# Causal masks as stack rows and small triangles, value products over two slots

## What is computed

```python
# L0 cross (its own half is causal), L2 feed-forward's attention
att = jnp.where(causal[None, None], att, -jnp.inf)
# L2 attention: three passes, each output is the next query
mask = jnp.triu(jnp.full((S, S), -10000.0), 1)
scores = jnp.einsum('bthd,bshd->bhts', q, k * scale) + mask
for _ in range(REPETITIONS - 1):
    context = _self_attention(context, k, v, mask)
```

## Time and profile before

| | |
|---|---|
| three runs | 4332.91, 4342.0, 4346.76 us, median 4342.0 |
| the profiled execution | span 4397.2 us; the time around it isn't shown, and it is an execution of its own beside the three |
| mean granted TensorE clock | 0.867 |
| busy over the span | PE 78%, PEld 51%, DVE 64%, ACT 47%, POOL 27% |
| instructions | 86721 |

### The profile page before, as it was taken

One profiled execution on the slowest core, in us unless ns is written; L12 is line 12 of the kernel. 1 busy time (PEld: TensorE's weight loads), 2 busy tenths in 40 slices (PEclk: granted clock), 3 DMA queues, 4 the chain that ended last, 5 costly groups with the idle time before them and its releaser, 6 DMA issues. The chain is left out here.

```text
span 4397.2 us, 86721 instructions
## 1 busy us (share of the span) xinstructions
PE 3437.7 (78%) x30670; PEld 2240.3 (51%) x30670; DVE 2793.4 (64%) x7633; ACT 2088.0 (47%) x4656; POOL 1182.3 (27%) x2276
## 2 busy tenths in 40 slices
PE   6886888896888658759998989677993588869882
PEld 2443554463555338734454545343553466669882
DVE  5884675264786575547676777476865468954453
ACT  2664665232443435426666766443660234335551
POOL 2322221011111234540101110133322422234555
PEclk9987998797998679969999999787995599879996
DMA  5323331033221322230202021223322230122322
GB/s 89 64 35 55 56 56 22 15 95 49 32 39 14 57 70 67 76 58 21 42 24 38 25 38 27 37 53 54 55 35 65 80 92 19 59 70 85 91 80 62
DMA packets 320664, 231.40 MB, mean 53 GB/s; under 512 B 45491, under 2 KB 305168, under 8 KB 320188
## 3 DMA queue, kind: packets, MB, share of 16 engines
q1 hardware_dynamic: 306444, 198.57, 22.8%
q0 software_dynamic: 12928, 26.50, 2.1%
q10 hardware_dynamic: 864, 0.79, 0.1%
HBM read 68.43 MB, written 55.53 MB: 28 GB/s over the span
## 5 line engine op out<-in xcount | busy, mean ns | idle before, releaser
L1373 ACT ACTIVATE PT<-ps 128x512 f32<-128x512 f32 (+1 forms) x1600 | 812.2, 559 | 468.7 <-PE ps L1433 223.0
L1323 DVE TENSOR_REDUCE M<-ps 128x2 f32<-128x512 f32 x1024 | 655.3, 684 | 236.1 <-PE ps L1307 209.3
L1286 PE MATMUL ps<-SKB 49*128 49x256 bf16 (+2 forms) x3584 | 422.6, 275 | 131.7 <-DVE M L1323 53.5
L1320 DVE TENSOR_REDUCE M<-ps 128x3 f32<-128x384 f32 x768 | 390.6, 550 | 180.5 <-PE ps L1304 119.5
L1468 PE MATMUL ps<-PT,VA 128*9 128x256 f32 (+1 forms) x7168 | 449.8, 370 | 1.3 <-ACT PT L1373 1.0
L3847 ACT ACTIVATE SKB<-ps,SKB 128x128 f32<-128x128 f32 x1032 | 295.5, 372 | 279.6 <-PE ps L3765 194.6
L1413 PE MATMUL ps<-SKB 51*128 51x256 bf16 (+2 forms) x3584 | 362.6, 267 | 59.4 <-DMA SKB<-MT 37.0
L3911 DVE COPY SKB<-SKB 128x1028 f32 (+1 forms) x258 | 186.6, 723 | 287.0 <-PE ps L3774 167.7
L1286 PEld LDWEIGHTS ps<-SKB 48*128 48x128 bf16 (+1 forms) x3584 | 137.8, 95 | 427.9 <-issue 131.0
L3774 PE MATMUL ps<-SKB 128*128 128x128 f32 x2064 | 288.7, 285 | 29.9 <-ACT SKB L3847 22.1
L3765 PE MATMUL ps<-SKB 128*128 128x128 f32 x2064 | 293.4, 288 | 0.0
(11 more groups left out here) (497 smaller groups left out, 6720.8 us busy)
## 6 DMA issues: line engine op xcount, KB each, us to landing
SKB<-HH SPq DMA_DIRECT2D x1212, 64.0 KB
SKB<-HH SPq DMA_DIRECT2D x576, 32.0 KB
PT<-L_sorted_rows SPq DMA_DIRECT2D x258, 64.0 KB
L_sorted_results<-SKB SPq DMA_DIRECT2D x258, 64.0 KB
SKB<-in_L3f_w SPq DMA_DIRECT2D x32, 256.0 KB
L_sorted_rows<-TV SPq DMA_DIRECT2D x2, 4032.0 KB, 29.4
SKB<-scratch SPq DMA_DIRECT2D x2, 2048.0 KB, 11.0
SKB<-in_L1f_w SPq DMA_DIRECT2D x16, 256.0 KB
```

Source lines behind the costliest of these rows:

```text
L1286: k = e.matmul(self.mx_bank(m + i)[:, o:o + n], K.QS[self.set(c)][64 * i:64 * i + rows, s, 256 * bb + 128 * qt:256 * bb + 128 * qt + 128], ...
L1320: k = e.tensor_reduce(K.M3[n % 2][:, hh, 0:3], mx[:, 0:384].rearrange("p (a k) -> p a k", a=3), axis=AX.X, op=ALU.max)
L1323: k = e.tensor_reduce(K.M3[n % 2][:, hh, 0:2], mx.rearrange("p (a k) -> p a k", a=2), axis=AX.X, op=ALU.max)
L1373: e.activation(K.PT[:, x % 4, n * i:n * i + n], self.st_bank(x, i)[:, 0:n], ACT.Exp, bias=0.0, scale=self.scale).then_inc(*self.exp.inc())
```

## The change

Masks. Behind the 48 rows of a head's stack come three mask rows, then the two ones rows (shift). Key row j is 0 up to key 64j + 63 and masked behind; query row j is 1 for queries 64j to 64j + 63. So the products that are made anyway mask all but four 64 x 64 triangles on the diagonal. `pe_triangle` adds these: per head two products with 64 rows (the head's own half of the array; an identity shifted by 64 columns in `idh`) and 128 columns, in place of one with 128 rows and 256 columns. The mask of the maxima now stands right behind the maxima. Value products are divided: the first key tile one slot earlier than before, the second where both were.

Copies. The 13 row patterns are made by DVE at the begin in one partition of X, written to DRAM in slot 30 of s0 (`sp_table`), and each stage copies its rows from there ahead of its first three stacks. `sp_mask_rows`, `sp_ones` and the loads of two masks at the begin and of one with the weights of s6 go.

```diff
+        self.idh = [sb(f"idh{i}", [128, 128], BF16) for i in range(2)]
+        self.tri = sb("tri", [128, 4, 64], BF16)
...
+    def sp_table(self, e):
+        K = self.K
+        e.wait_ge(*self.patterns.at(0))
+        for r in range(13):
+            e.dma_start(K.row_table[r:r + 1, :].rearrange("p (b k) -> p b k", b=16),
+                        K.X[0:1, r:r + 1, :].to_broadcast([1, 16, 128])).then_inc(self.tabled.sem, 16)
+
     def sp_rows(self, e, c):
         K = self.K
+        if c == 0:
+            e.wait_ge(*self.tabled.at(0))
...
+        for i, words in enumerate((A["c_maskq"][0:64, 0:32], A["c_maskk"][0:64, 0:32], A["c_addm"][0:64, 0:32],
+                                   A["c_addm"][0:64, 128:160])):
+            for par in range(2):
+                e.dma_start(K.tri[64 * par:64 * par + 64, i, :].bitcast(F32), words).then_inc(self.late.sem, 16)
...
         e.tensor_copy(K.idb[:, :], K.idf[:, :]).then_inc(*self.set.inc())
+        self.dve_patterns(e)
+
+    def dve_patterns(self, e):
+        K = self.K
+        rows = K.X[0:1, 0:13, :].bitcast(BF16)
+        for at, value in ((0, NEG), (5, MASKED)):
+            for j in range(3):
+                e.memset(rows[:, at + j, 0:64 * j + 64], 0.0)
+                e.memset(rows[:, at + j, 64 * j + 64:256], value)
+            e.memset(rows[:, at + 3:at + 5, :], 1.0)
+        for j in range(3):
+            if j > 0:
+                e.memset(rows[:, 10 + j, 0:64 * j], 0.0)
+            e.memset(rows[:, 10 + j, 64 * j:64 * j + 64], 1.0)
+            e.memset(rows[:, 10 + j, 64 * j + 64:256], 0.0)
...
-        self.mrow = 49 if mode == "add" else 48
+        self.mrow = 51 if self.masked else 48
...
+            if step == 0 and key < 3:
+                self.sp_stack_rows(e, kind, key)
...
+    def sp_stack_rows(self, e, kind, c):
+        K, i = self.K, self.set(c)
+        if kind == "q":
+            at, n, dst = 10, 3 * self.masked, K.QS[i]
+        elif self.masked:
+            at, n, dst = 5 * (self.mode == "add"), 5, K.KS[i]
+        else:
+            at, n, dst = 3, 2 * (self.begin is None), K.KS[i]
+        for par in range(2 if n else 0):
+            r = 64 * par + 48
+            e.dma_start(dst[r:r + n, :, :].bitcast(F32), K.row_table[at:at + n, :].rearrange("r (a k) -> r a k", a=8)
+                        ).then_inc(self.rows_in[i].sem, 16)
...
+    def pe_triangle(self, e, bank, i, sub, turned):
+        K = self.K
+        if self.mode == "causal":
+            blocks = bank.rearrange("p (a k) -> p a k", a=2)
+        else:
+            blocks = bank.rearrange("p (a k) -> p a k", a=4)[:, 0:4:3, :]
+        part = slice(64 * i, 64 * i + 64)
+        tri = K.tri[part, 2 * (self.mode == "add") + turned:2 * (self.mode == "add") + turned + 1, :].to_broadcast([64, 2, 64])
+        return e.matmul(blocks[:, :, 64 * sub:64 * sub + 64], K.idh[sub][part, :], tri, start=False, stop=sub == 1)
...
     def pe_max_mask(self, e, u, s):
         K, mode = self.K, self.mode
-        if mode == "none":
+        if self.masked:
+            for sub in range(2):
+                for i in range(2):
+                    k = self.pe_triangle(e, self.mx_bank((16 + 4 * self.cross) * u + 2 * s + i), i, sub, 0)
+                    if sub == 1:
+                        k.then_inc(*self.mx.inc())
+        if mode != "bias":
             return
...
     def pe_exp_mask(self, e, u, s):
...
+        if self.masked:
+            for sub in range(2):
+                for i in self.heads(x):
+                    k = self.pe_triangle(e, self.st_bank(x, i), i, sub, 1)
+                    if sub == 1:
+                        k.then_inc(*self.st.inc())
...
-    def pe_pv(self, e, u, j):
+    def pe_pv(self, e, u, j, kt):
...
-        if j % 2 == 0 and f > 0:
+        if kt == 0 and j % 2 == 0 and f > 0:
             e.wait_ge(*self.tv.at(f - 1))
...
-        e.wait_ge(*self.exp_done(x + 1))
+        if kt == 0:
+            e.wait_ge(*self.exp_done(x + 1))
...
+        if kt == 1:
+            k.then_inc(*self.pv.inc())
...
+        if maxima and self.masked:
+            self.pe_max_mask(e, *maxima)
         if scores:
             self.pe_exp(e, *scores)
-        if maxima:
+        if maxima and not self.masked:
             self.pe_max_mask(e, *maxima)
...
         for j in range(4):
-            u = self.at(g, LE + 2 * j + 3)
-            if u is not None:
-                self.pe_pv(e, u, j)
+            for kt in range(2):
+                u = self.at(g, LE + 2 * j + 2 + kt)
+                if u is not None:
+                    self.pe_pv(e, u, j, kt)
...
+        if self.begin and g == 30:
+            self.begin.sp_table(e)
```

More of the change, by code:

```diff
@@ L929, in sp, with __init__ @@
         e.dma_start(K.BIG[96:100, 0:8192], K.A["c_kc"]).then_inc(self.kone.sem, 16)
-def twice(mask):
-    return mask.rearrange("p (o k) -> p o k", o=1).to_broadcast([128, 2, 128])
 class SelfAttention(Heads):
     LE, MBT, CMBT, TV, GATE = 12, 9, 11, (5, 9, 11), 8
-    def __init__(self, K, prev, W, mode, rope=False, reps=1, gate=False, cross=False, kind="ln", g=None, lead=0, ring=0, again=False,
-                 begin=None):
+    def __init__(self, K, prev, W, mode, rope=False, reps=1, gate=False, cross=False, kind="ln", g=None, lead=0, ring=0, begin=None):
         self.K, self.prev, self.W, self.mode, self.rope = K, prev, W, mode, rope
@@ L974, in __init__ @@
         self.rope_tables = (W["rc"], W["rs"]) if rope else None
-        self.mask = W["mask"].bitcast(BF16) if mode == "add" else None
-        self.mrow = 49 if mode == "add" else 48
+        self.masked = mode in ("causal", "add")
+        self.mrow = 51 if self.masked else 48
         self.MX = (0, 1) if mode == "bias" else (0, 1, 5)
@@ L982, in __init__ @@
         self.scale_q = RS8 / self.scale
-        self.rows_in = K.ev("mask_rows_in", 1, 16 * 18) if mode == "add" else None
-        self.ones_in = K.ev("ks_ones_in", 1, 16 * 6) if again else None
+        self.rows_in = [K.ev(f"stack_rows{i}", 1, 16 * (4 if self.masked else 0 if begin else 2)) for i in range(3)]
         nff = len(self.ff_splits) - 2 * cross
@@ L1278, in pe_max @@
                 e.wait_ge(*self.stacked.at(self.split_of["k", c]))
+                if c < 3 and not self.begin:
+                    e.wait_ge(*self.rows_in[self.set(c)].at(0))
         parts = [(0, 0, 128), (1, 128, 256)] if self.causal else [(0, 0, 256), (1, 256, 256)]
@@ L1456, in pe_pv @@
         x = self.nx * u + 2 * j
-        if j % 2 == 0 and f > 0:
+        if kt == 0 and j % 2 == 0 and f > 0:
             e.wait_ge(*self.tv.at(f - 1))
-        if j == 0 and bb == 0 and self.units[u][1] == 0:
+        if kt == 0 and j == 0 and bb == 0 and self.units[u][1] == 0:
             e.wait_ge(*(self.vact if self.W["vb"] is None else self.vdve).at(c))
-        e.wait_ge(*self.exp_done(x + 1))
+        if kt == 0:
+            e.wait_ge(*self.exp_done(x + 1))
         g = j % 2
-        for kt in range(2):
-            for i in range(4):
-                lo = 128 if kt == 1 and self.causal else 0
-                o = 256 if kt == 1 else 0
-                pt = K.PT[:, (x + i // 2) % 4, 0:2 * self.width].rearrange("p (a k) -> p a k", a=2)
-                k = e.matmul(K.PS[32 * i:32 * i + 9, 6, 256 * g + lo:256 * g + 256],
-                             K.VA[self.set(c)][:, (2 * bb + kt) * 16 + 8 * (i % 2) + 2 * j + i // 2, :], pt[:, i % 2, o:o + 256 - lo],
-                             start=kt == 0, stop=kt == 1)
-        k.then_inc(*self.pv.inc())
+        lo = 128 if kt == 1 and self.causal else 0
+        o = 256 if kt == 1 else 0
+        for i in range(4):
+            pt = K.PT[:, (x + i // 2) % 4, 0:2 * self.width].rearrange("p (a k) -> p a k", a=2)
+            k = e.matmul(K.PS[32 * i:32 * i + 9, 6, 256 * g + lo:256 * g + 256],
+                         K.VA[self.set(c)][:, (2 * bb + kt) * 16 + 8 * (i % 2) + 2 * j + i // 2, :], pt[:, i % 2, o:o + 256 - lo],
+                         start=kt == 0, stop=kt == 1)
+        if kt == 1:
+            k.then_inc(*self.pv.inc())
     def pe_gate(self, e, u):
@@ L1534, in pe @@
         self.join(e)
-        if self.mode == "add":
-            e.wait_ge(*self.rows_in.at(0))
-        if self.ones_in:
-            e.wait_ge(*self.ones_in.at(0))
         for g in range(self.lead, self.slots):
@@ L2297, in sp_slot @@
                 self.later.load(e)
-            if self.next is not None and self.next.ones_in:
-                self.next.sp_ones(e)
         if self.beside is not None:
@@ L4509, in program @@
         s7 = CrossAttention(K, s6, W[7], kind="rms", g=K.g8[:, 0:1], lead=28)
-        s8 = SelfAttention(K, s7, W[8], "causal", rope=True, kind="keep", g=K.g8[:, 1:2], lead=28, ring=2,
-                           again=True)
+        s8 = SelfAttention(K, s7, W[8], "causal", rope=True, kind="keep", g=K.g8[:, 1:2], lead=28, ring=2)
         g9 = Gates(K, s8, W[9], 8, "L2", top=2)
```

71 lines of the change are left out of this document (20 added, 51 removed).

## The result

Four runs of the changed kernel took 4299.08 to 4314.79 us, median 4309.3; the four of before 4332.91 to 4346.76, median 4342.2. The ratio is 0.993, 95% interval 0.9911 to 0.995: faster, by 33 us, where 69 were forecast. The profiled execution of after spans 4313.0 us at a mean granted clock of 0.857 (before 4397.2 and 0.867). Most of the 84 us between the two spans lies outside the five stages: from the last slot of s8 to the end, where nothing is changed, it is 1126 us before and 1081 after. That tail follows the machine and not the kernel: it is 1111 to 1116 us in e5 to e8, which ran on one chip together, and 1079 to 1085 in the other experiments. So stages are compared, not spans.

The account below looks back on a forecast made before the run. PE was taken as first bound in s1, s6 and s8, with copy loops and queues in s6's later passes and s1. Terms -44 - 24 - 18 + 3 + 2 + 2 + 10 = -69 us took 4342 to 4273, range 4220 to 4325.

Parts of the forecast that it names:

- The division: Value products halved into every slot: with the masks' new order, shape changes per two slots five to four, 0.09 us gained.
- s8: Stage s8: 1.5 us gained per unit of 2.1 less PE work, DVE being next; 24 us over 16 units.
- s1: Stage s1: about 2 us per pair of units where PE holds, copies holding the rest; 18 us gained.
- s0 and s3: Stages with unchanged masks: 17 us more PE work from shape changes, mostly behind DVE; 3 us lost, bounds -10 and 17.
- Triangles: Masks in s1, s6, s8: paired triangles take 0.22 us per slot instead of 0.45; gain 0.23, bounds 0 and 0.23.
- The new wait: First half of value products waits for the preceding slot's exponentials; 0 to some 0.6 us behind a TV copy, taken as 0.
- First passes of s6: PE holds these units of s6; 1.6 us gained per unit of 2.1 less PE work, DVE next at 13.5.
- Later passes: In s6 a loop of stack copies and ACT's work holds the units; 0.4 us gained per unit, more where copies queue.
- The clock: Idler PE lowers the granted clock; 10 us lost, bounds 0 and 30, under 0.9 in s6 a sign of error.
- A: Rival: copies keep nearly all, s6's later passes and s1 don't move, s8 gives half; 4321 us, chance 0.12.
- C: Rival: mask pairs don't run side by side, only shape changes are gained; 4344 us, chance 0.06.
- D: Rival: slower through the clock, break-even at granted 0.84 in s1, s6 and s8; 4420 us at 0.75, chance 0.06.

Follow-up runs that it names:

- e5: Changed kernel with the twelve stack copies between passes of s6 moving one row of eight each (output not the reference's); s6 769 us, single run.
- e8: Changed kernel with value products whole and the maxima's triangles behind the score products again; ratio 0.9946 against before.
- e4: Changed kernel with value products divided in s6 and s8 only, whole in s0, s1 and s3; ratio 0.9869 against before.
- e1: Kernel before with the value products divided over two slots and nothing else; ratio 1.0076 against before.
- e2: Changed kernel with value products whole in one slot as before, so the masks alone; ratio 0.9904 against before.
- e11: Changed kernel with the maxima of s6 reduced over every second key (output not the reference's); ratio 0.9918 against before.
- e3: Changed kernel with twelve overwritten products ahead of each unit's first maxima in second and third passes of s6; ratio 0.9922 against before.
- e10: Changed kernel with value products divided in s6 alone and twelve overwritten products per unit in its later passes; 4270.2 us, ratio 0.9831 against before.

## Why the prediction was half right

The direction, the range (4220 to 4325) and the mechanism of the masks held; the size didn't, 33 us of 69. Two steps failed. The division was booked as a small gain on PE and 3 us of loss in s0 and s3, with none in s1, and it costs 26 us in these three stages (after against e4). And in s6 PE's work fell as forecast, by 100 us or 2.1 per unit, but only 26 us of 44 arrived. By its own terms, in the profiled executions:

| term | forecast | measured |
|---|---|---|
| s6 | -44 | -26 |
| s8 | -24 | -12 |
| s1 | -18 | +5 |
| s0 and s3 | +3 | -5 and +13 |
| begin, first slot of s0 | +2 | +2 |
| copies | +2 | not told apart from s0 |
| clock, in the stages | +10 | 9 in s6, 6 in s1, won back by fillers |

The measured stage rows hold the clock already. Together they give -23 us; the medians say -33. No run places the 10 us between the two: each row is from one execution of either kernel.

*Triangles, right.* 0.11 us for four, no whole-array product left in a slot. Products and masks came to 0.77 us from 1.09, 0.32 gained per slot; I had 0.23 and, per two slots, one change of shape.

*The division, the term that failed.* I counted changes of shape before and after as a balance, five to four, and with 2.1 us per unit booked a small gain. That hid that the triangles, which have the maxima's own shape, take three away and the division adds two. One part paid for the other. For s3 I had worked out 6 us of PE time and for s0 11, and took 3 together because DVE is busy 83% of s0. Measured, s3's busy time grew by 13.2 us in e1, 12.2 of it PE work at full clock, and 10 us came onto the path: an average of 83% says nothing about the slots that hold turns and projections, where PE is behind. In s0 nothing of it was seen, -2 in e1 and -5 in after. In s1, whose slots have cross-attention and so more whole-array steps, I had no charge at all; there the division cost 18 us between e2 and after, 9 of it PE work and 12 slower clock, against 2 less idle time. The fillers gave 6 back. A pair of units of s1 takes 47.0 us where I had 42 and before has 44.4, with the shift wait kept (2.7 at most). The rule that I had weighed and set aside, that a change of the tiling mode drains the engine (the Trainium skill, "TensorEngine Tiling (Array Packing)", section Tiling Modes), agrees with the runs: by it the division was a loss of 0.7 per unit, and e1 shows 0.91 in s8 and 0.7 in s1 and s3.

*The new wait, nearly right.* Taken as 0, bounds 0 and 0.6 behind a TV copy. Value products wait for the exponentials of the slot before six times in eight units of s3, 1.8 us in all; for TV 37 times in the 48 units of s6, 12.4 us, 0.3 each, some 0.26 per unit that the sum lacks.

*First passes of s6, mis-sized.* 1.6 per unit forecast. Over all of them, from one unit's first maxima to the next's, 16.8 became 16.0; in the four units of the earlier trace rows 17.0 became 16.7. In those PE's time fell by 63.26 - 57.33 = 5.9 us in four units, 1.5 of the 2.1 per unit, and its idle time rose from 4.8 to 9.4. The floor that I gave for DVE, 13.5 per unit, isn't what holds (e11); the waits take turns.

*Later passes, the loop right and the gain wrong.* The loop holds them: 15.1 us per unit at full clock, with a wait for the last stack copy of 1.23 us above, where I had 15.4 and over 1. But only 9 of 31 take less than 15.2. Over all units second passes took 16.3 us in place of 16.1, so they didn't gain the 0.4, and third passes 17.3 in place of 18.3. The price that I didn't see is that the waits for stack copies, 13.9 us in s6 before and 52.9 after, lower the clock at the start of many units. With the fillers of e3 second passes take 15.5.

*s8, mis-sized.* 0.8 per unit in place of 1.5: 16.8 to 16.0. The masks alone give as much (236 us), so the division isn't at fault here: over all of s8 it costs 9 us of PE work at full clock, and 4 of idle time and 4 of slower clock go. With both edits PE work fell by 22 us where 34 were booked, since the division takes part of what the masks give.

*The clock, too small or about right, by how it is counted.* 10 us, bounds 0 and 30. The lower clock stretched PE's busy time by 31 us more than before in s6 and 15 in s1; the fillers win 15 back in the two. How much of the rest lay on the path isn't shown. The place was wrong: I named 0.9 in s6 as the alarm, and s6 kept 0.92, while s1 fell to 0.88.

Of the rivals, A, at 4321, is nearer in time than the forecast's 4273, and in good part for its reasons: the second passes of s6 didn't get shorter, and s8 gave half. But third passes did get shorter, first passes gave half of its 1.6 per unit, and s1 didn't stand still, it paid for the division. C, that pairs don't pair, is refuted by the timeline. D, the clock, came in part, and its 0.84 wasn't reached in s1 or s6.

## What to carry to other kernels

Price each edit of a bundle by itself, with a sign, before netting it: here one of two cancelled a good part of the other, and dropping it outside the stage that it helps, with fillers, more than doubled the gain. Count transitions between shapes of the used array as work of TensorE, ahead of and behind each group, and charge them in the slots where TensorE is late, not by the stage's busy share. Before busy times of two runs are compared, take out what the clock did to them. Where a saving turns into a wait at a fixed place, look at what the clock does behind it.

## What the runs showed of the hardware

- A small group of products in another shape of the array costs 0.09 us on the way in and 0.12 on the way out: 0.31 against 0.22 us from a mask to the next step, and 0.55 + 0.34 against 0.77 us for the divided and the whole value products in s8.
- Behind a wait of 2.32 us products ran at the lower clock for about 6 us (four maxima products 0.61 us in place of 0.39); behind one of 1.23 us they didn't. Twelve products whose result is thrown away, ahead of each such wait, brought 9 us in s6 (e3 against the change) and 13 (e10 against e4) although they are work.
- Issuing twelve stack copies took SP 8.06 us when each moved one row of eight and 7.90 when it moved all: here the issue is paid by the copy, not by the byte.
- A reduction over 256 strided values per partition took 0.42 us and one over 512 in a row 0.68, so about 0.16 of either isn't for the values, if the stride costs nothing.
